# A decoder on one core: hyperbolic projection and attention in one stage, and three pairs of banks for the last head group

## The reference

```python
def L0_xattn(x, cross_input, ...):               # 16 heads of 16
    att  = q @ k.T * scale;  causal               # self attention, causal
    y    = softmax(att) @ v
    y    = y + softmax(qc @ kc.T * scale) @ vc    # cross attention, 1024 keys
    return y @ Wp + bp

def L1_attn(x, ...):                              # hyperbolic attention
    spikes = sigmoid(x @ w_sur + b_sur) > threshold
    q, k, v = heads(x @ W_qkv + b_qkv)
    def expmap0(u):
        n = sqrt(max(-u[0]**2 + sum(u[1:]**2), 1e-8))
        return cosh(n), sinh(n) * u[1:] / n
    neg_inner = einsum(tq, tk) - einsum(sq, sk)
    dist   = arccosh(max(neg_inner, 1 + 1e-7))
    scores = where(causal, -dist**2 / sqrt(D), -inf)
    return (softmax(scores) * spikes) @ v @ W_out + b_out

def mha(x, y, ..., causal):                       # last block, 16 heads of 32
    a = softmax(q @ k.T * D**-0.5)
    if causal: a = a * (key > query)              # masked after the softmax
    x_out = x + (a @ v) @ li1_w + li1_b
    return x_out + gelu(ln(x_out) @ li2_w + li2_b) @ li3_w + li3_b
```

## Time and profile before

| | |
|---|---|
| median of 3 runs | 3841.73 us (3839.04 to 3848.53) |
| profiled execution, its own time | 3852.28 us |
| its span | 3850.5 us |
| mean granted TensorE clock | 0.935 of full speed |
| PE, DVE, ACT, POOL busy | 85%, 54%, 43%, 24% |
| instructions | 57114 |

### The profile page before, as it was taken

How to read it: one execution, slowest core, us unless ns; L and a number is a source line. 1 busy time by engine, 2 the same in 40 slices (tenths; PEclk the granted TensorE clock), 3 DMA queues, 4 the chain that set the end, 5 groups by cost and what they waited for, 6 DMA issues and landing times. The chain is left out here.

```text
span 3850.5 us, 57114 instructions
## 1 busy us (share of the span) xinstructions
PE 3279.7 (85%) x21920; PEld 1798.1 (47%) x21920; DVE 2066.1 (54%) x4278; ACT 1651.3 (43%) x2497; POOL 916.9 (24%) x966
## 2 busy tenths in 40 slices
PE   6888788899898788898897788999897788975997
PEld 4325445235325545244335535254335535254997
DVE  5575655644666664635656664635656665732111
ACT  3353933343354833343345742433356642431332
POOL 1202912011203712011204622011105522023111
PEclk9899799999998899999998899999998898985998
DMA  4113021111203022011203022011211022025997
GB/s 123 38 33 83 1 47 66 49 34 45 58 13 82 1 47 93 21 38 49 60 10 76 1 47 93 21 39 47 62 44 39 1 47 93 22 89 194 333 327 243
DMA packets 250142, 270.61 MB, mean 70 GB/s; under 512 B 96198, under 2 KB 215988, under 8 KB 247572
## 3 DMA queue, kind: packets, MB, share of 16 engines
q1 hardware_dynamic: 202288, 207.46, 18.5%
q10 hardware_dynamic: 44180, 50.17, 4.1%
q0 software_dynamic: 3408, 9.34, 0.6%
HBM read 199.87 MB, written 67.05 MB: 69 GB/s over the span
## 5 line engine op out<-in xcount | busy, mean ns | idle before, releaser
L881 ACT ACTIVATE prob<-psum 128x1024 f32<-128x1024 f32 x384 | 372.2, 1021 | 513.3 <-PE psum L799 513.3
L1262 ACT ACTIVATE prob<-psum 128x1024 f32<-128x1024 f32 (+3 forms) x384 | 331.2, 914 | 367.7 <-PE psum L1151 367.7
L927 DVE TENSOR_REDUCE scr<-psum 128x1 f32<-128x512 f32 x576 | 369.4, 685 | 198.9 <-PE psum L786 195.0
L1304 DVE TENSOR_REDUCE stats<-psum 128x1 f32<-128x512 f32 (+3 forms) x576 | 332.2, 619 | 143.6 <-PE psum L1139 140.5
L796 PE MATMUL psum<-stack 32*128 32x512 f32 x1536 | 226.6, 660 | 15.3 <-ACT prob L881 10.4
L1139 PE MATMUL psum<-stack 96*128 96x512 bf16 (+3 forms) x576 | 183.8, 367 | 31.5 <-DVE stats L1304 31.2
L412 PE MATMUL psum<-ident 128*128 128x128 f32 x1664 | 204.9, 278 | 2.7 <-ACT stack L2222 2.7
L412 PEld LDWEIGHTS psum<-ident 128*128 128x128 f32 x1664 | 197.1, 193 | 15.0 <-issue 7.5
L829 PE MATMUL psum<-prob,ones_f 128*32 128x512 f32 x1536 | 203.4, 598 | 0.0
L1166 PE MATMUL psum<-prob,vbig 128*32 128x512 f32 (+3 forms) x1536 | 191.1, 570 | 0.0
L1693 POOL TENSOR_TENSOR xo<-xa,rows 128x256 f32<-128x256 f32 x32 | 22.2, 725 | 660.3 <-POOLq L69 660.3
(11 more groups left out here) (489 smaller groups left out, 6381.9 us busy)
## 6 DMA issues: line engine op xcount, KB each, us to landing
ew<-in_L_ffn_W SPq DMA_DIRECT2D x39, 1024.0 KB, 6.7
ew<-in_L_ffn_W ACTq DMA_DIRECT2D x39, 1024.0 KB, 7.9
stack<-q_terms SPq DMA_DIRECT2D x144, 128.0 KB, 2.6
w_mlp<-in_L_xattn_a_li_w SPq DMA_DIRECT2D x16, 1024.0 KB, 6.5
q_terms<-parts SPq DMA_DIRECT2D x96, 128.0 KB, 2.2
stack<-k_terms SPq DMA_DIRECT2D x72, 128.0 KB, 3.0
stack<-k_terms SPq DMA_DIRECT2D x36, 256.0 KB, 4.3
w_mlp<-a_terms SPq DMA_DIRECT2D x36, 256.0 KB, 5.0
```

Source lines behind the costliest of these rows:

```text
L881: act.activation(prob[:, i % 4, :, :], psum[:, 2 * p:2 * p + 2, :], ACT.Exp, scale=scale).then_inc(exped, 1)
L927: dve.tensor_reduce(found[:, c:c + 1], ring(i), AX.X, ALU.max).then_inc(freed, 1)
L1262: act.activation(prob[:, i % 4, :, q0:T], psum[:, 2 * p:2 * p + 2, q0:T], ACT.Exp, scale=scale).then_inc(exped, 1)
L1304: dve.tensor_reduce(found[:, c:c + 1], ring(i)[:, 0:keys_of(t)], AX.X, ALU.max).then_inc(freed, 1)
```

## The change

1. **Three pairs of banks.** `score_bank` gives the steps of the last head group the pairs 0-1, 2-3 and 4-5 in turn, two heads to a pair; `exps_before_score` lets `score(n)` wait there for one exponential less. This holds for `Ba`, `Bca`, `e1` and `e2`.
2. **Joins.** `join_attention` writes to banks 6 and 4 instead of 4 and 5. The pairs lie at `kt` 4, 5 and 6 (behind a wait for the division of group 2), one pair before the last `gather`, one behind it, and one behind `spread_inverses`, where the filler matmuls fall from 6 to 2. `fp6_linear` follows with its banks.
3. **One stage.** `De` and `Da` become one `nc.Block`. The first group's strips are turned and copied tile by tile, q and k together (`turn_first`), into banks 7 and 6; `score(0)` stands behind the second tile. The strips of groups 1 to 3 are turned in six halves (`turn_half`), each one bank, one per round of PE's loop behind a score that is due, and copied by `take_half`. The values are added (`value`) and the spike computed (`fire`) inside DVE's loop. The table with Exp and Ln is loaded once, in place of two loads.

```diff
+    def score_bank(n, j, kts):
+        m = n - (HG - 1) * kts
+        return j if m < 0 else 2 * ((2 * m + j // 2) % 3) + j % 2
+
+    def exps_before_score(n, kts):
+        return 2 * n if n <= (HG - 1) * kts else 2 * n - 1
...
                     if n:
-                        pe.wait_ge(exped, 2 * n)
+                        pe.wait_ge(exped, exps_before_score(n, kts))
...
-                        pe.matmul(psum[:, j, :], KTg[W * j:W * j + W, g, kt * P:(kt + 1) * P], QTg[W * j:W * j + W, g, :],
+                        pe.matmul(psum[:, score_bank(n, j, kts), :], KTg[W * j:W * j + W, g, kt * P:(kt + 1) * P], QTg[W * j:W * j + W, g, :],
...
-                        act.activation(prob[:, i % 4, :, :], psum[:, 2 * p:2 * p + 2, :], ACT.Exp, scale=scale).then_inc(exped, 1)
+                        b0 = score_bank(n, 2 * p, kts)
+                        act.activation(prob[:, i % 4, :, :], psum[:, b0:b0 + 2, :], ACT.Exp, scale=scale).then_inc(exped, 1)
...
-                    if next_products and g == HG - 1 and 3 <= kt < 7:
-                        pe.wait_ge(divided, HG - 2)
-                        for t, k in next_products[2 * kt - 6:2 * kt - 4]:
+                    if next_products and g == HG - 1 and 4 <= kt < 7:
+                        pe.wait_ge(divided, HG - 1)
+                        for t, k in next_products[2 * kt - 8:2 * kt - 6]:
                             join_attention(pe, t, k)
...
-                if next_products:
-                    pe.wait_ge(divided, HG - 1)
-                for t, k in next_products[8:10]:
+                for t, k in next_products[6:8]:
...
-                keep_running(pe, 6, 3)
+                for t, k in next_products[10:]:
+                    join_attention(pe, t, k)
+                keep_running(pe, 2 if next_products else 6, 3)
...
-        return pe.matmul(psum[:, 4 + t // 2, t % 2 * C:(t % 2 + 1) * C], yT[:, k, t * P:(t + 1) * P], wBp[:, k, :],
+        return pe.matmul(psum[:, (6, 4)[t // 2], t % 2 * C:(t % 2 + 1) * C], yT[:, k, t * P:(t + 1) * P], wBp[:, k, :],
...
+            def turn_half(n):
+                g, i = strip_halves[n]
+                pe.wait_ge(first_in, QT)
+                if n >= 2:
+                    pe.wait_ge(strips_in, n - 1)
+                for t in range(QT):
+                    last = turn_strip(pe, i, g, t * P, 6 + n % 2, t)
+                last.then_inc(strips, 1)
+
+            def turn_first(t):
+                if t == 1:
+                    pe.wait_ge(imp_in, 1)
+                if t >= 2:
+                    pe.wait_ge(first_in, t - 1)
+                for i, built in enumerate((q_wide, k_wide)):
+                    pe.wait_ge(built, t + 1)
+                    last = turn_strip(pe, i, 0, i * P, 7 - t % 2, t)
+                last.then_inc(first_strips, 1)
...
+            turn_first(0)
+            turn_first(1)
             score(0)
-            turn_strips(1)
-            turn_strips(2)
+            turn_first(2)
+            turn_first(3)
             for i in range(-2, NU + 8):
                 if i + 2 < NU and i + 2 in last_unit and units[i + 2][0] + 1 < len(quads):
                     score(units[i + 2][0] + 1)
-                if i == 0:
-                    turn_strips(3)
+                if 0 <= i + 2 < len(strip_halves):
+                    turn_half(i + 2)
...
             for i in range(-2, NU + 9):
                 if i + 2 < NU:
                     above_one(i + 2)
+                if 0 <= i + 1 < QT:
+                    value(i + 1)
+                if i == SLOTS:
+                    fire()
...
+            act.wait_ge(least, 1)
+            act.activation(nroot, nmin, ACT.Sqrt).then_inc(rooted, 1)
+            act.preload_act_table_set("natural_log_exp_and_others")
...
+            for t in range(QT):
+                act.wait_ge(first_strips, t + 1)
+                act.copy(both[:, :, 0, t * P:(t + 1) * P],
+                         psum[:, 7 - t % 2, 0:2 * P].rearrange("p (i n) -> p i n", i=2)
+                         ).then_inc(first_in, 1)
+
+            take_half(0)
             for i in range(NU + 3):
...
+                if i == 3:
+                    act.wait_ge(imp_in, 1)
+                    act.activation(spike, imp, ACT.Exp, scale=-1.0).then_inc(spike_e, 1)
+                if i < 3:
+                    for n in ((1, 2), (3, 4), (5,))[i]:
+                        take_half(n)
```

More of the change, by code:

```diff
@@ L2136, in standard_attention @@
                    stack[:, 4096:12288].rearrange("p (s j n) -> p s j n", s=2, j=J), add=e.colB[:, 0, :], ready=2,
-                   next_products=[(t, k) for k in range(HG - 1) for t in range(QT)], beside=add_bias)
+                   next_products=[(t, k) for t in range(QT) for k in range(HG - 1)], beside=add_bias)
 def fp6_linear(e):
@@ L2200, in _ @@
                 pe.wait_ge(quant, h + 1)
-                turn(h, 6 + h).then_inc(turned, 1)
+                turn(h, 5 + 2 * h).then_inc(turned, 1)
             for h in range(2):
@@ L2484, in by_head @@
         return v[:, 0:units[i][4] * keys(i)].rearrange("p (j n) -> p j n", n=keys(i))
-    with stage(nc, "Da", "scored", "over", "wready", "logged", "rooted", "summed", "far", "squared_dve", "squared_act", "exped", "keep_in", "keep_ready", "turned",
-               "copied", "weighed", "dc", "lifted", "gathered", "inverted", "spread_in", "divided", "strips", "strips_in") as (
-            block, scored, over, wready, logged, rooted, summed, far, squared_dve, squared_act, exped, keep_in, keep_ready, turned,
-            copied, weighed, dc, lifted, gathered, inverted, spread_in, divided, strips, strips_in):
+    strip_halves = [(g, i) for g in range(1, HG) for i in range(2)]
@@ new lines, in hyperbolic_attention @@
+    with stage(nc, "Da", "qk_summed", "v_summed", "raw_in", "squared", "zeros", "dc_map", "imp_in", "least", "rooted",
+               "both_exped", "mapped", "q_wide", "k_wide", "first_strips", "first_in", "spike_e", "v_in",
+               "scored", "over", "wready", "logged", "wrooted", "summed", "far", "squared_dve", "squared_act",
+               "exped", "keep_in", "keep_ready", "turned", "copied", "weighed", "dc", "lifted", "gathered",
+               "inverted", "spread_in", "divided", "strips", "strips_in") as (
+            block, qk_summed, v_summed, raw_in, squared, zeros, dc_map, imp_in, least, rooted, both_exped, mapped,
+            q_wide, k_wide, first_strips, first_in, spike_e, v_in, scored, over, wready, logged, wrooted,
+            summed, far, squared_dve, squared_act, exped, keep_in, keep_ready, turned, copied, weighed, dc,
+            lifted, gathered, inverted, spread_in, divided, strips, strips_in):
@@ new lines, in _ @@
+            for i in range(1, 5):
+                for dst, terms in series:
+                    last = dve.scalar_tensor_tensor(dst, dst, 1.0 / terms[i], below_one, ALU.add, ALU.mult)
+                then_mapped(last)
+            for dst, terms in series:
+                last = dve.tensor_scalar(dst, dst, 1.0, None, ALU.add)
+            dve.tensor_scalar(pick, nmin, 1.0, None, ALU.is_lt)
+            dve.wait_ge(rooted, 1)
+            then_mapped(dve.reciprocal(per_root, nroot))
+            dve.wait_ge(both_exped, 2)
@@ L2677, in _ @@
                     exponentiate(i - 3)
+        @block.sync
+        def _(sp):
+            e.load_qkv(sp, 1)
         @block.gpsimd
```

253 lines of the change are left out of this document (106 added, 147 removed).

## The result

The kernel after takes 3797.6 us (median of four runs, 3789.4 to 3799.7); the kernel before, run beside it, 3842.5. The ratio of the runs is 0.9878 with a 95% interval of 0.9858 to 0.9897: 1.2% faster. A second measurement gave 0.9886 (0.9871 to 0.9901). The forecast was 3801.

A forecast was written before the change was run, and what follows sets the result against it. No engine is full over the span; four batches pass through stages, each with its own limit. 4 x (2.9 + 1.1 + 1.5 + 1.6 + 2.0) + 1.6 + 2.4 = 40.4 us, 1.05% off the median 3841.73: 3801, range 3783 to 3818.

The forecast's parts named there:

- The shorter wait in the last groups: Last head groups: scores wait one exp half less; per batch cross 2.9, causal 1.1, last block's self 1.5, cross 1.6 us.
- The tail's cover, at 0: Cross attention's tail: the join pair moved there hides beside DVE's last two instructions, costing 0; without cover 1.06 us.
- The clock, 1.6 + 2.4 = 4.0: Low-clock stretches after idle gaps: 1.6 us back in cross attention's batch 0, half of three others (2.4) in causal attention.
- The joined stage, 2.0 a batch: Hyperbolic stages joined: ACT's dense stream starts earlier; chain gives 3.1 once, 2.3 in three batches, taken as 2.0, bounds 0 and 4.
- First reduction at about 4.1: Sign in the joined stage: DVE's first reduction about 4.1 us after the last copy_predicated.
- Log 1 3 to 4.5 earlier: Sign in the joined stage: ACT's log of unit 1 comes 3 to 4.5 us earlier, relative to the last copy_predicated.
- If ACT waited for halves for more than 2 us: Sign in the joined stage that would show the prediction wrong: ACT waiting over 2 us for strip halves.
- POOL's unit 4: Joined stage: POOL's unit 4 waits for all six halves until about 382.4, before its turn in the old order (387).
- Rival 3: Three pairs of banks do nothing, PE already sets the pace; only the joined stage's 8 us left; 3834; chance 0.05.
- rival 4: Low clock takes the joined stage, PE bounds it at 150 for 132; 44 us slower in all, 3886; chance 0.05.
- rival 1: Joined stage's early start eaten by ACT waiting for halves: gives 0 or loses 1 us; 3806 to 3810; chance 0.18.
- Rival 2: More than counted: all low-clock stretches vanish and the joined stage gives 4 a batch; 51 us won, 3791; chance 0.12.

The follow-up runs named there:

- Experiment 3: Kernel after, but scores in the last head group wait again for both exp halves of the score before; 3827.4 us, ratio 0.9971 to the kernel before.
- experiment 8: Kernel after with one more pair of joins moved from cross attention's last group into its tail; 3788.2 us, ratio 0.9856 to the kernel before.
- experiment 9: Kernel after with two more pairs of joins moved from cross attention's last group into its tail; 3793.8 us, ratio 0.987 to the kernel before.
- experiment 2: Kernel before with only the joined hyperbolic stage of the kernel after; 3829.1 us, ratio 0.9977 to the kernel before.
- Experiment 4: Kernel after without the 22 filler matmuls on PE ahead of the joined stage's first turned tile; 3800.7 us, ratio 0.9887 to the kernel before.
- experiment 6: Kernel after with the stage boundary back, score 0 after all four first tiles, all else kept; 3814.3 us, ratio 0.9926 to the kernel before.
- experiment 7: Kernel after with four strip halves turned in a block behind the first tiles, two behind later scores; 3794.3 us, ratio 0.9874 to the kernel before.
- experiment 1: Kernel after with the kernel before's separate hyperbolic stages; three pairs, early wait and moved joins kept; 3800.1 us, ratio 0.9892 to the kernel before.
- experiment 5: Kernel after, unchanged, measured and profiled once more; 3796.6 us, ratio 0.9886 to the kernel before.
- experiment 10: Kernel after with two of four matmuls repeated where row maxima are measured (cross attention, last block); 3830.4 us, ratio 0.9963 to the kernel before.

## Why the prediction was right, point by point

*The shorter wait in the last groups* was priced at 7.1 a batch and gave, by windows and without the clock, 3.08 + 1.05 + 1.5 + 1.7 = 7.3. Cross attention: 2.9 forecast, 3.08 found (step 2.29 for 2.23, step with joins 3.13 for 3.20). Causal attention: 1.1 forecast, 1.05 found in the batch with the full clock. Self attention: 1.5 and 1.5. Last cross attention: 1.6 and 1.7. Experiment 3 shows that the wait is the cause.

*The tail's cover, at 0*: right; the tail is 7.62 in both, and experiments 8 and 9 show where the cover ends.

*The clock, 1.6 + 2.4 = 4.0*: found 4.54 - 3.08 = 1.46 in cross attention's batch 0, and 1.94 - 1.05 = 0.89 in each of three batches of causal attention, 4.1 in all. That it would be half of it there was a guess; all three batches gave the same value.

*The joined stage, 2.0 a batch*: by its windows this is the mis-sized term of the sum. Those of the first execution gave 5.75 once and 3.4 three times, 16.0 for 8. In the median the stage alone gave 8 to 9 (experiment 2), the price on record, so what follows is about the window. Two things were wrong in it. The chain put log 1 at 12.15 after the mark, with PE's durations between the two clocks; it came at 10.33 because PE, with no boundary to stand at, ran the ramp at the full clock. Experiment 4 took the clock away and log 1 came at 13.4; experiment 6 put the boundary back and it came at 15.25 to 15.66, about the value of before. And I lowered the chain's 2.3 to 3.1 to 2.0 as "fragile", where the third distance came 4.0 to 5.1 earlier. What followed the ramp, ACT full from the fourth log, was right: from log 4 to log 15 the kernels before and after need 46.1 and 45.4.
That PE keeps or loses its clock by what it did before is what the Trainium skill, page "TensorE: Matmul & The Clock Gate", section "Part 1: The HAM clock gate", states. The fear drawn from it, that the stage would run colder without its dense block, was not borne out (0.82 to 0.83 after, 0.79 to 0.81 before).

*The signs.* First reduction at about 4.1: 3.72. Log 1 3 to 4.5 earlier: 4.9 and 6.2, outside, by the same error. "If ACT waited for halves for more than 2 us" was a bad sign: it waited 1.41, 1.05, 0.79 and 0.73, 4.0 together in batch 0, and the stage won more than forecast. These waits did hold up the first logs: POOL's square of unit 1 ended at 361.86, and its log began at 362.85, behind two halves. But experiment 7 takes four halves ahead of the first log, has log 1 2 to 3.5 later, and at best the same log 4: how often ACT stops for a half says little, and its idle time in sum up to log 4, 4.0 in both, is what counts. POOL's unit 4, said to be free before its turn, waited 0.90 for the halves at 369.83; no later work shows it.

*The rivals.* None came true. Rival 3 is refuted by experiment 1, rival 4 by the granted clock, rival 1 (start eaten) by log 4 at 22.05 where before had 25.5 to 26.4. (Its sum on record is wrong: 40.4 less the stage's 8, or less 12, leaves 28 to 32, not 32 to 36.) Rival 2 had 4 for the stage and all of the clock: 3791. The windows are near it (49.4 of its 51), the median is not.

*Why the median was still close.* By windows the change is worth 49.4, by medians 44.9. Experiments 1 and 2 say on which side: the pairs give 37 to 41 where their windows hold 33, the stage 8 to 11 where its window holds 14 to 17 (and beside the pairs, by the ratio to experiment 1, 2 to 5). That the sum fell near the forecast of 40.4 is in part luck: pairs that pay more than their price of 32 met a stage that pays less than its window. Between the profiled executions of experiments 1 and 5, which differ by the stage, 13.9 us won in it stand against 8.6 more in three untouched stretches (behind causal attention, ahead of the last cross attention, between the batches). Over the four batches these three come to 1191 in the kernel before, to 1187 and 1191 in experiments 1 and 6, which lack the joined stage too, and to 1184 to 1209 in the nine traces that have it and no repeated matmuls. Whether the joined stage causes that or the executions merely fell so, these can't tell. It stays open.

One thing in it is clear: a stretch of which no instruction was changed need not keep its length. Ahead of the last cross attention (from the end of self attention's last group to cross attention's first ob copy) the four batches take 513.2 to 514.7 in the three traces with the old wait (before, experiments 2 and 3) and 503.1 to 507.9 in the nine with the short wait and no repeated matmuls. Between the batches (from the last group's end to the next batch's first ob copy, three stretches) it is the other way, 389.4 to 390.6 and 393.4 to 399.5. Why is not shown; in sum the two nearly cancel.

## What to carry to other kernels

A stage boundary costs more than the time over which the engines stand: here 1.2 us of standing, 1.8 for work that has to wait for all of the stage before it, and 1.9 through TensorE's clock in the work that follows, so price what comes behind a removed boundary at the higher clock. Where a chain is paced by two engines handing over to each other, count the wait in halves: one more pair of banks and one exponential less were worth the whole idle time, the banks by themselves nothing. When a part's window and its effect on the median disagree, run the part alone before the sum is believed.

## What the runs showed of the hardware

**One stretch, two lengths, in the same program.** From causal attention's last ob copy to cross attention's first it is 71 to 74.3 us in most batches, and 80.4 to 85.0 in 6 of the 56 batches of the fourteen profiled executions. In the execution of experiment 2, batch 3 had 80.45 and batch 2 had 72.06. Windows of PE, the first two in batch 2, the next four in batch 3 (length, PE busy, granted clock, DMA share, GB/s):

```profile
1881.00:1891.00 10.00, 7.21 (x42) 1.00 0.62 176
1891.00:1901.00 10.00, 7.72 (x48) 1.00 0.33 101
...
2725.00:2735.00 10.00, 8.73 (x33) 0.59 0.67 176
2735.00:2745.00 10.00, 9.18 (x31) 0.50 0.20 73
2745.00:2755.00 10.00, 8.92 (x33) 0.54 0.00 0
2755.00:2765.00 10.00, 9.60 (x63) 1.00 0.27 74
```

and three windows at the low clock, one in batch 2 and two in batch 3:

```profile
1870.20:1877.00 6.80, 6.24 (x19) 0.50 0.26 51
2709.90:2713.20 3.30, 3.15 (x16) 0.50 0.68 194
2726.90:2754.10 27.20, 24.96 (x78) 0.50 0.27 73
```

For some 27 us PE ran at 1.2 GHz while it was busy nine tenths of the time, and the group was 8.4 us longer. The instructions are the same in both batches, and so are PE's waits up to the first short fall of the clock. That fall lies 22.4 us behind causal attention's last ob copy and lasts 6.8 in batch 2, and lies 18.4 behind it and lasts 3.4 in batch 3; only batch 3 falls again, for the 27 us. So the code alone doesn't decide, and filling most of PE's idle time where the row maxima are measured (experiment 10) did not prevent it. The Trainium skill, page "TensorE: Matmul & The Clock Gate", section "Part 1: The HAM clock gate", says that activity restores the clock; in these rows PE was busy nine tenths of the time, with work that lasts twice as long at that clock (a score 2.09 for 1.14), and the clock did not come back for 27 us. All twelve runs of experiment 2 lie in two heaps, 3823 to 3830 and 3835 to 3843, a distance of about one such stretch; that it is this stretch which divides them is not shown, as one execution only has a trace.

**The ramp's clock too differs from batch to batch.** In experiment 8, whose joined stage is that of the kernel after to the instruction, log 1 came at 11.83 in two batches and at 10.32 in the two others. Score 2 found the low clock there: 1.66 where it takes 0.93. Timeline of PE:

```profile
355.58 0.71 PE L2417 MATMUL psum<-stack 32*128 32x256 f32 x8
356.22 0.66 PE L2321 MATMUL psum<-ident,stack 128*128 128x128 f32 x4
357.97 0.58 PE L2413 MATMUL psum<-hide_below,identb 128*128 128x128 bf16 x4 [1.09 <-DVE vbig L2515]
358.49 1.66 PE L2417 MATMUL psum<-stack 32*128 32x384 f32 x8
```

The same section of that page of the Trainium skill says that the number of matmuls which run at the low clock varies from run to run of one kernel. The two executions of the kernel after agree: in batch 2 log 1 came at 10.32 in the first and at 11.75 in experiment 5.

**The first execution of a program**, the profiled one, was the slowest of its runs in 9 of 14 cases. That of the kernel before was the slowest of its own, that of the kernel after the fastest: read two profiles by stretches, not by their ends.
